# A gated graph network: first block tile by tile, catching up over four blocks, and a new split of low parts in the last layer

## The chip, the cores and the metric

The kernel runs on one core of one Trainium2 chip. The time is the device time of the whole program in microseconds (us); the profile shows one execution of it.

## What is computed

Four layers of a gated graph network on 50,000 nodes with 128 features, and a layer norm over each node's features at the end. With the self loops that the input carries there are 75,000 edges, sorted by destination; 25,000 of the edges are not self loops.

```python
def gru(inp, h):
    i_r, i_z, i_n = split(inp @ w_ih.T + b_ih)
    h_r, h_z, h_n = split(h @ w_hh.T + b_hh)
    r, z = sigmoid(i_r + h_r), sigmoid(i_z + h_z)
    n = tanh(i_n + r * h_n)
    return (1 - z) * n + z * h
h = x
for l in range(4):
    m = h @ weight[l]
    agg = segment_sum(m[src], dst, 50000)
    h = gru(agg, h)
out = layernorm(x + (h + x))
```

## The kernel before

Nodes are taken in 100 blocks of 500 (NB = 100), four to a partition row. A block's state stands transposed, features on partitions and 504 columns (COLS), and each float32 operand of a matmul is split in a high part, rounded on ScalarE (h_hi, g_hi, a_hi), and a low part, the rest, subtracted on VectorE or GpSimd (h_lo, g_lo, a_lo). A product is then three matmuls. weight[l] is folded into w_ih ahead of the loops, so a layer works on the sum of neighbours' states.

A block's other edges lie in three tiles of at most 128 (TILES = 3), one for each third of its rows. GpSimd gathers the sources' rows (gath, L570, three indirect DMAs a block, issued five blocks ahead), and TensorE adds them up by a product with a 0/1 selection (sel) into the PSUM tensor pA (sum_edges, L689: six matmuls of 168 columns). VectorE adds the block's own state (aggT, L1161); in the last layer TensorE does that with two passes through an identity matrix, and aggT does not exist. pA holds one block's sums, so the next sum waits until these are read: for aggT (s_agg), in the last layer for a_lo (s_alo).

Each engine runs an order written out by hand, one step for each block b of each layer, and semaphores tie the engines together. In step b:
- TensorE: r and h_n products on the state of b, r and i_n products on the sums of b, the edge sum of b + 2, the z products of b, the transposes of the new state of b - 1 (L764).
- ScalarE: r gate of b (rg, L892), h_hi and g_hi of b + 3, tanh (L896), a_hi of b + 2, z gate; in the last layer also two halves of the normalised rows of b - 9 (L914), in the others the copy of the rows of b - 2.
- VectorE: narg = h_n times r (L1167), newT of b - 1 (L1193), narg + i_n (L1174), in the last layer the residual sum y_rows of b - 2 (L1202) and its row statistics bn (L1209), in the others aggT of b + 2; then diff = h - n (L1178), g_lo of b + 3 (L1140), in the first three layers the second half of h_lo of b + 3 (L1145), a_lo of b + 2 (L1152), diff times z (L1184). The moments of five blocks are worked out together, once in five steps. In the first layer VectorE also makes the selections (L1129), four blocks ahead.
- GpSimd: h_lo of b + 3 (L550; the first half, in the last layer all 504 columns), the three gathers of b + 5, and in the last layer once in five steps a root for the row norms (L556).
- SP issues loads and stores. Rows go out through a ring of five buffers, o_rows.

A layer's gathers read the rows that the layer before has stored, so its first gather waits for the last store. The steady step has the edge sum two blocks ahead, and a layer begins with none: block 0 is summed alone (L779), the first three steps (RAMP) sum one block ahead, and the third of them sums a second one at its end (L793). The other engines follow with g_hi, g_lo, aggT, a_hi and a_lo in the same places. After the last step the last nine blocks' rows are normalised, the first half of each on ScalarE (L979), the second on VectorE (last_rows, L1317), into o_rows; both wait until the buffer's last store is done.

The branch on flag takes the path described here; general_path is for inputs that don't fit the tables and isn't run.

## Time and profile before

| | |
|---|---|
| median of the three runs | 2383.14 us (lowest 2382.7) |
| the profiled execution's own time | 2381.4 us |
| its span, first to last instruction | 2379.7 us |
| TensorE matmul busy | 2239.1 us (94%) |
| TensorE weight load busy | 1885.0 us (79%) |
| VectorE busy | 2233.1 us (94%) |
| ScalarE busy | 1900.6 us (80%) |
| GpSimd busy | 1724.1 us (72%) |

Matmuls overlap and their ends are modelled, so a TensorE that is busy may still not be at its peak: what it can do is better read from the starts of its instructions. In rows of the time line an instruction's duration holds some 0.09 us after the point at which the next one may start. "issue" is time in which the profile shows nothing that the engine waited for. Names as DVE, ACT, POOL, PE and SP stand for VectorE, ScalarE, GpSimd, TensorE and the SyncE queue.

### The profile page before, as it was taken

Reading aid. Unit: us, or ns where it says so; the run is one execution under the profiler, and the core shown is the slowest. Engines: PE = TensorE matmul, PEld = TensorE weight load, DVE = VectorE, ACT = ScalarE, POOL = GpSimd, SP = SyncE. Lnnn points to the kernel's source line nnn. Section 1 sums busy time; section 2 is a strip of 40 time slices with the busy share of each in tenths; the row PEclk is TensorE's granted clock in tenths of the full one; section 3 lists DMA queues with packets and bytes.
Section 4 is the critical chain, followed back from the end, with each engine's and each line's share of the span. In section 5 each row is a group of like instructions: output and inputs, shape, how many; then the busy total and the mean of one; then the engine's idle time right before and its main releaser. Section 6 shows DMA issues by size and latency. Waiting matters only on the chain.

```text
span 2379.7 us, 49508 instructions
## 1 busy us (share of the span) xinstructions
PE 2239.1 (94%) x11832; PEld 1885.0 (79%) x11832; DVE 2233.1 (94%) x4543; ACT 1900.6 (80%) x3592; POOL 1724.1 (72%) x1645
## 2 busy tenths in 40 slices
PE   2799999999989999999979999999979999999996
PEld 1688888888768888888858888888858888888885
DVE  7799999999879999999969999999969999999998
ACT  1588888888768888888858888888857999999996
POOL 2687777777376777777567777777658888888883
PEclk7899999999989999999989999999989999999998
DMA  2355555555546555555535555555544555555553
GB/s 57 89 158 162 158 161 157 161 157 161 154 115 173 172 172 169 174 172 169 169 112 174 170 173 172 169 172 173 169 124 122 153 151 150 151 151 151 151 152 110
DMA packets 277065, 363.68 MB, mean 153 GB/s; under 512 B 107755, under 2 KB 186587, under 8 KB 276981
## 3 DMA queue, kind: packets, MB, share of 16 engines
q1 hardware_dynamic: 238196, 310.43, 43.7%
q0 software_dynamic: 38784, 52.30, 9.0%
q8 instruction: 32, 0.52, 0.1%
q14 instruction: 53, 0.43, 0.1%
HBM read 209.32 MB, written 179.81 MB: 164 GB/s over the span
## 4 chain that ended last, share of the span: by engine, by line
DVE 48%; issue 29%; PE 10%; ACT 9%; DVEq 2%; DMA 1%; POOL 0%; SPq 0%; ACTq 0%; POOLq 0%
DVE a_lo L1152 9%; DVE narg L1174 8%; DVE diff L1178 5%; DVE h_lo L1145 5%; DVE diff L1184 5%; ACT pA L896 3%; ACT pIN L896 3%; PE pR L717 3%; DVE aggT L1161 3%; DVE sel L1129 3%; PE pA L705 2%; DVE newT L1193 2%; DVE narg L1167 2%; PE pZ L717 2%; DVE bn L1209 2%
## 5 line engine op out<-in xcount | busy, mean ns | idle before, releaser
L570 POOL DMA_INDIRECT gath<-state,idx x900 | 943.6, 1048 | 260.0 <-issue 239.7
L550 POOL TENSOR_TENSOR h_lo<-hT,h_hi 128x252 fp32r<-128x252 f32 (+1 forms) x400 | 351.7, 879 | 247.1 <-ACT h_hi L869 162.6
L570 POOL DMA_INDIRECT gath<-in_x_dram,idx x300 | 345.7, 1152 | 108.6 <-issue 72.1
L892 ACT ACTIVATE rg<-pR,bsum 128x504 f32<-128x504 f32 x400 | 272.5, 681 | 87.3 <-PE pR L717 75.6
L1167 DVE SCALAR_TENSOR_TENSOR narg<-pHN,bhh,rg 128x504 f32<-128x504 f32 x400 | 294.0, 735 | 31.4 <-ACT rg L892 29.6
L705 PE MATMUL pA<-sel,g_hi 128*128 128x168 f32 x1200 | 278.4, 266 | 22.3 <-DVE g_lo L1140 22.3
L705 PE MATMUL pA<-sel,g_lo 128*128 128x168 f32 x1200 | 291.3, 276 | 0.0
L880 ACT CAST sel<-sel 128x504 fp32r (+1 forms) x400 | 246.3, 616 | 34.1 <-DVE flag_i L1136 33.9
L1184 DVE TENSOR_TENSOR diff<-zg,diff 128x504 f32<-128x504 f32 x400 | 270.3, 676 | 0.8 <-DVE diff L1178 0.5
L900 ACT ACTIVATE zg<-pZ,bsum 128x504 f32<-128x504 f32 x400 | 269.9, 675 | 0.0
L1140 DVE TENSOR_TENSOR g_lo<-gath,g_hi 128x384 fp32r<-128x384 f32 x400 | 231.7, 579 | 35.8 <-ACT g_hi L873 35.8
L705 PEld LDWEIGHTS pA<-sel,g_hi 128*128 128x128 f32 x1200 | 231.3, 193 | 41.6 <-issue 25.1
L705 PEld LDWEIGHTS pA<-sel,g_lo 128*128 128x128 f32 x1200 | 231.5, 193 | 16.4
L896 ACT ACTIVATE pA<-narg,bih 128x504 f32<-128x504 f32 x200 | 137.2, 686 | 134.2 <-DVE narg L1174 133.6
L764 PEld LDWEIGHTS pO<-ident,newT 128*125 128x125 f32 x1400 | 197.2, 187 | 56.3 <-DVE newT L1193 30.2
L896 ACT ACTIVATE pIN<-narg,bih 128x504 f32<-128x504 f32 x200 | 137.2, 686 | 127.4 <-DVE narg L1174 126.7
L873 ACT CAST g_hi<-gath 128x384 fp32r<-128x384 f32 x400 | 207.4, 518 | 24.7 <-DMA gath<-state,idx 23.0
L764 PE MATMUL pO<-ident,newT 128*125 128x128 f32 x1400 | 215.3, 276 | 11.0 <-DVE newT L1193 11.0
L1152 DVE TENSOR_TENSOR a_lo<-aggT,a_hi 128x504 fp32r<-128x504 f32 x300 | 203.4, 678 | 2.7 <-ACT a_hi L885 2.7
L1161 DVE TENSOR_TENSOR aggT<-pA,hT 128x504 f32<-128x504 f32 x300 | 200.7, 669 | 5.0 <-PE pA L705 5.0
L885 ACT CAST a_hi<-aggT 128x504 fp32r<-128x504 f32 x300 | 179.4, 598 | 17.2 <-DVE aggT L1161 17.2
L717 PE MATMUL pR<-h_hi,whh_hi 128*128 128x504 f32 x400 | 191.2, 478 | 0.0
(185 smaller groups left out, 6460.7 us busy)
## 6 DMA issues: line engine op xcount, KB each, us to landing
columns<-newT SPq DMA_DIRECT2D x300, 252.0 KB, 2.0
hT<-columns SPq DMA_DIRECT2D x300, 252.0 KB, 2.7
state<-o_rows SPq DMA_DIRECT2D x300, 224.0 KB
x_rows<-in_x_dram SPq DMA_DIRECT2D x200, 224.0 KB
out_dram<-o_rows SPq DMA_DIRECT2D x100, 224.0 KB
gath<-state,idx POOLq DMA_INDIRECT x900
state<-o_rows SPq DMA_DIRECT2D x300, 26.0 KB
idx<-edge_src SPq DMA_DIRECT2D x395, 1.5 KB
```

The costliest lines, as they stand in the source:

```text
L550: nc.gpsimd.tensor_tensor(h_lo[:, u % RING, cols], hT[:, u % RING, cols], h_hi[:, u % RING, cols].bitcast(F32), ALU.subtract).then_inc(s_h ...
L570: pool.indirect_dma_start(out=gath[:, u % RING, j, :], out_offset=None, in_=states[l], in_offset=bass.IndirectOffsetOnAxis(ap=idx[:, u % R ...
L705: last = nc.tensor.matmul(to, rows, cols, start=begins, stop=ends)
L717: last = nc.tensor.matmul(bank, w, xx[:, u % RING, :], start=begins and k == 0, stop=ends and k == len(passes) - 1)
L764: last = nc.tensor.transpose(bank[0:ROWS, k * D:(k + 1) * D], newT[:, u % RING, k * CP:k * CP + ROWS], ident[:, :])
L892: nc.scalar.activation(rg[:, :], pR[:, 0:COLS], ACT.Sigmoid, bias=bsum[:, 0:1]).then_inc(s_r, 1)
L896: nc.scalar.activation(n_bank(u), narg[:, :], ACT.Tanh, bias=bih[:, 2:3]).then_inc(s_n, 1)
L900: nc.scalar.activation(zg[:, :], pZ[:, 0:COLS], ACT.Sigmoid, bias=bsum[:, 1:2]).then_inc(s_z, 1)
L1152: v.tensor_tensor(a_lo[:, u % RING, :], sums_of if summed else aggT[:, :], a_hi[:, u % RING, :].bitcast(F32), ALU.subtract).then_inc(s_alo, 1)
L1161: v.tensor_tensor(aggT[:, :], sums_of, hT[:, u % RING, :], ALU.add).then_inc(s_agg, 1)
L1167: v.scalar_tensor_tensor(narg[:, :], pHN[:, 0:COLS], bhh[:, 2:3], rg[:, :], ALU.add, ALU.mult).then_inc(s_t1, 1)
L1184: v.tensor_tensor(diff[:, :], zg[:, :], diff[:, :], ALU.mult).then_inc(s_e, 1)
```

## The change

**First block, tile by tile.** Each of the three gathers of a layer's block 0 gets its own semaphore. g_hi, g_lo, the two matmuls, aggT, a_hi and a_lo run for each tile (128 gathered columns, 168 block columns) in three PSUM banks (first_sums), by the new functions first_gathered and first_high_part on ScalarE and first_low_gathered, first_aggregate and first_low_part on VectorE, each the old work on a third of the columns.

**Catching up over four blocks.** RAMP is 4. Steps 0 to 2 sum blocks 1 to 3; step 3 sums block 4 between the r and the i_n product and block 5 behind the z products. g_hi, g_lo and a_lo of these blocks, VectorE's part of h_lo and the selections move to match; block 1's g_hi and g_lo, made ahead of step 0 before, are made in it.

**Last layer.** GpSimd makes 378 columns of h_lo (MOST) and VectorE the other 126; the state products and the edge sum wait for both. g_lo of b + 3 stands between the residual sum and the row statistics.

**Ends.** In a layer's last step newT of the block before goes ahead of narg, and h_lo behind the last newT. The last nine blocks are normalised in place, in y_rows, and stored from there: ScalarE takes all columns of the first four of them, and half of the other five; the shift of the earlier group stands ahead of the last moments.

```diff
 HALF = COLS // 2
+MOST = 3 * COLS // 4
...
-RAMP = 3
+RAMP = 4
...
             for k in range(OUTLAG, 0, -1):
-                sp.wait_ge(s_olast, OUTLAG - k + 1)
-                store(l, NB - k, UNROLL - k)
+                if k <= RING:
+                    sp.wait_ge(s_olast, RING - k + 1)
+                store(l, NB - k, UNROLL - k, True)
...
 def split_h(l, b, u, behind=None, whole=False, ready=1):
-    cols = slice(0, COLS if whole or l == L - 1 else HALF)
+    cols = slice(0, COLS if whole else MOST if l == L - 1 else HALF)
...
     if l == L - 1:
         pe.wait_ge(s_hlo, g + 1)
+        pe.wait_ge(s_hlov, g + 1 - PRE)
...
-def products_on_sums(l, b, u, reused):
+def sum_first(l, start):
+    at_least(s_alo if l == L - 1 else s_agg, l * NB, start)
+    if l == L - 1:
+        pe.wait_ge(s_hlo, l * NB + 1)
+        pe.wait_ge(s_hlov, l * NB + 1 - PRE)
+        for j in range(TILES):
+            nc.tensor.matmul(first_sums(j), ident_r[:, :], of_rows(h_hi[:, 0, :], j), start=True, stop=False)
+            nc.tensor.matmul(first_sums(j), ident_r[:, :], of_rows(h_lo[:, 0, :], j), start=False, stop=False)
+    pe.wait_ge(s_sel, l * NB + 1)
+    for j in range(TILES):
+        pe.wait_ge(*of_first(j, s_ghi0, s_ghi, l))
+        nc.tensor.matmul(first_sums(j), g_hi[:, 0, j, :], selection(0, j), start=l < L - 1, stop=False)
+        pe.wait_ge(*of_first(j, s_glo0, s_glo, l))
+        nc.tensor.matmul(first_sums(j), g_lo[:, 0, j, :], selection(0, j), start=False,
...
-            products_on_state(l, b, u, start, l < L - 1 and (l > 0 or exists_before(i, u, PRE)))
+            products_on_state(l, b, u, start, l > 0 or exists_before(i, u, PRE))
             if first:
-                sum_edges(l, 0, 0, start)
+                sum_first(l, start)
                 z_on_state(l, 0, 0, start)
-            products_on_sums(l, b, u, l * NB + b - 1 if l or exists_before(i, u, 2) else None)
-            if exists(i, u, 2):
-                sum_edges(l, *after(i, u, 1 if ramp else 2)[:2], False)
+            r_on_sums(l, b, u)
+            if ramp and u == 3:
+                sum_edges(l, 4, 4, False)
+            n_on_sums(l, b, u, l * NB + b - 1 if l or exists_before(i, u, 2) else None)
+            if ramp and u == 2:
+                sum_edges(l, 3, 3, False)
+            elif not ramp and exists(i, u, 2):
+                sum_edges(l, *after(i, u, 2)[:2], False)
             if first:
                 z_on_sums(l, u)
             else:
                 z_product(l, b, u, start)
+            if ramp and u != 2:
+                nu = 5 if u == 3 else u + 1
+                sum_edges(l, nu, nu, False)
             if not first:
...
+def normalise_in_place(u, shifted, columns):
+    act.wait_ge(s_nmr, shifted)
+    for k in range(columns):
+        row = y_rows[:, u, k * D:(k + 1) * D]
+        last = nc.scalar.activation(row, row, ACT.Identity, bias=nmr[:, u, k:k + 1], scale=rstd[:, u, k:k + 1])
+    last.then_inc(s_o, 1)
 def fast_path():
     for l in range(L):
...
 def low_h(l, b, u):
     dve.wait_ge(s_hhi, l * NB + b + 1)
-    v.tensor_tensor(h_lo[:, u % RING, HALF:COLS], hT[:, u % RING, HALF:COLS],
-                    h_hi[:, u % RING, HALF:COLS].bitcast(F32), ALU.subtract).then_inc(s_hlov, 1)
+    cols = slice(MOST if l == L - 1 else HALF, COLS)
+    v.tensor_tensor(h_lo[:, u % RING, cols], hT[:, u % RING, cols], h_hi[:, u % RING, cols].bitcast(F32),
+                    ALU.subtract).then_inc(s_hlov, 1)
...
             if first:
                 if l == 0:
-                    for j in range(TILES):
-                        select(1, 1, j)
-                low_gathered(l, 0, 0)
-                if l == 0:
-                    for j in range(TILES):
-                        select(2, 2, j)
+                    for c in range(1, RAMP):
+                        for j in range(TILES):
+                            select(c, c, j)
+                first_low_gathered(l, 0)
                 if not final:
-                    aggregate(l, 0, 0, l == 0)
-                low_part(l, 0, 0, final)
-                low_gathered(l, 1, 1)
-                if l == 0:
-                    for j in range(TILES):
-                        select(3, 3, j)
+                    first_aggregate(l, 0, l == 0)
+                first_low_gathered(l, 1)
+                first_low_part(l, 0)
+                if not final:
+                    first_aggregate(l, 1, l == 0)
+                first_low_gathered(l, 2)
+                first_low_part(l, 1)
+                if not final:
+                    first_aggregate(l, 2, l == 0)
+                first_low_part(l, 2)
             added = final and exists_before(i, u, ROWLAG)
             half = half_done(i, u, RING + ROWLAG) if final else None
             shifted = half_done(i, u, OUTLAG) if final else None
+            ramp = isinstance(i, int) and i == 0 and u < RAMP
+            if last:
+                renew(*after(i, u, -1))
             r_times_hn(l, b, u)
+            if ramp and u == 1:
+                low_gathered(l, 2, 2)
             if shifted:
                 shift(*shifted)
-            if not first:
+            if not first and not last:
                 renew(*after(i, u, -1))
             n_argument(l, b, u)
+            if ramp and u == 0:
+                low_gathered(l, 1, 1)
+            if ramp and u == 3:
+                low_gathered(l, 5, 5)
             if added:
                 remainder(*after(i, u, -ROWLAG))
+                if not ramp and exists(i, u, 3):
+                    low_gathered(l, *after(i, u, 3)[:2])
                 row_stats(*after(i, u, -ROWLAG)[:2])
-            ramp = isinstance(i, int) and i == 0 and u < RAMP
             summed = after(i, u, 1 if ramp else 2)[:2] if exists(i, u, 2) else None
+            if ramp and u == 0:
+                difference(l, b, u)
             if not final and summed:
                 aggregate(l, *summed)
             if half:
                 moments(*half, RING * (half[1] + 1))
-            if l == 0 and exists(i, u, 4):
+            if l == 0 and exists(i, u, RAMP) and not ramp:
                 for j in range(TILES):
-                    select(*after(i, u, 4)[:2], j)
-            difference(l, b, u)
+                    select(*after(i, u, RAMP)[:2], j)
+            if not (ramp and u == 0):
+                difference(l, b, u)
             if half:
                 squared_difference(*half)
-            if ramp and u == RAMP - 1:
-                low_gathered(l, RAMP + 1, RAMP + 1)
-            if not ramp and exists(i, u, 3):
+            if not added and not ramp and exists(i, u, 3):
                 low_gathered(l, *after(i, u, 3)[:2])
             coming = on_from(l, i, u, PRE)
-            if coming and coming[0] < L - 1:
+            if coming and not ramp and not last:
                 low_h(*coming[:3])
             if summed:
                 low_part(l, *summed, final)
+            if ramp and u == 3 and not final:
+                aggregate(l, 5, 5)
+            if ramp and u == 2:
+                low_gathered(l, 4, 4)
             product(l, b, u)
+            if coming and ramp:
+                low_h(*coming[:3])
             if half:
                 variance(*half)
-            if ramp and u < RAMP - 1:
-                low_gathered(l, u + 2, u + 2)
-            if ramp and u == RAMP - 1:
-                if not final:
-                    aggregate(l, RAMP + 1, RAMP + 1)
-                low_gathered(l, RAMP + 2, RAMP + 2)
-                low_part(l, RAMP + 1, RAMP + 1, final)
+            if ramp and u == 1:
+                low_gathered(l, 3, 3)
+            if ramp and u == 3:
+                low_part(l, 5, 5, final)
+                low_gathered(l, 6, 6)
+            if l == 0 and ramp:
+                for j in range(TILES):
+                    select(RAMP + u, RAMP + u, j)
             if last:
                 renew(b, u, i)
+                if coming:
+                    low_h(*coming[:3])
         blocks(dve, step)
         if final:
...
                 u = UNROLL - k
                 dve.wait_ge(s_nmr, turn(GROUPS - 1, u) + (1 if k > LATE else 2))
-                dve.wait_ge(s_store[u % RING], 32 * (TURNS * (L - 1) + turn(GROUPS - 1, u)))
                 for c in range(RPP // 2, RPP):
-                    last = v.tensor_scalar(o_rows[:, u % RING, c * D:(c + 1) * D], y_rows[:, u, c * D:(c + 1) * D],
-                                           rstd[:, u, c:c + 1], nmr[:, u, c:c + 1], ALU.mult, ALU.add)
+                    row = y_rows[:, u, c * D:(c + 1) * D]
+                    last = v.tensor_scalar(row, row, rstd[:, u, c:c + 1], nmr[:, u, c:c + 1], ALU.mult, ALU.add)
                 last.then_inc(s_olast, 1)
             ahead = slice(RING, UNROLL - LATE), TURNS - 1
...
             for k in range(LATE, 0, -1):
                 remainder(NB - k, UNROLL - k, GROUPS - 1)
                 row_stats(NB - k, UNROLL - k)
+            shift(*ahead)
             moments(*late, NB)
             squared_difference(*late)
             variance(*late)
-            for k in range(OUTLAG, RING, -1):
-                last_rows(k)
-            shift(*ahead)
             for k in range(RING, LATE, -1):
                 last_rows(k)
             shift(*late)
```

VectorE at the start of the second layer, before: g_lo, aggT and a_lo of block 0, g_lo of block 1, then the steps of blocks 0 and 1.

```order
L1140 TENSOR_TENSOR g_lo<-gath,g_hi 128x384
L1161 TENSOR_TENSOR aggT<-pA,hT 128x504
L1152 TENSOR_TENSOR a_lo<-aggT,a_hi 128x504
L1140 TENSOR_TENSOR g_lo<-gath,g_hi 128x384
L1167 SCALAR_TENSOR_TENSOR narg<-pHN,bhh,rg 128x504
L1174 TENSOR_TENSOR narg<-pIN,narg 128x504
L1161 TENSOR_TENSOR aggT<-pA,hT 128x504
L1178 TENSOR_TENSOR diff<-hT,pIN 128x504
L1145 TENSOR_TENSOR h_lo<-hT,h_hi 128x252
L1152 TENSOR_TENSOR a_lo<-aggT,a_hi 128x504
```

The same place after, from the second tile of block 0 on.

```order
L1271 TENSOR_TENSOR a_lo<-aggT,a_hi 128x4x42
L1264 TENSOR_TENSOR aggT<-pIN,hT 128x4x42
L1271 TENSOR_TENSOR a_lo<-aggT,a_hi 128x4x42
L1278 SCALAR_TENSOR_TENSOR narg<-pHN,bhh,rg 128x504
L1285 TENSOR_TENSOR narg<-pIN,narg 128x504
L1230 TENSOR_TENSOR g_lo<-gath,g_hi 128x384
L1289 TENSOR_TENSOR diff<-hT,pIN 128x504
L1252 TENSOR_TENSOR aggT<-pA,hT 128x504
L1243 TENSOR_TENSOR a_lo<-aggT,a_hi 128x504
L1295 TENSOR_TENSOR diff<-zg,diff 128x504
L1236 TENSOR_TENSOR h_lo<-hT,h_hi 128x252
```

g_lo of block 1 has moved from ahead of the step into it, diff stands ahead of aggT, and h_lo behind the second diff. The next piece is VectorE in a steady step of the last layer, before.

```order
L1193 TENSOR_TENSOR newT<-diff,pIN 128x504
L1174 TENSOR_TENSOR narg<-pA,narg 128x504
L1201 REGISTER_ALU
L1202 SCALAR_TENSOR_TENSOR y_rows<-x_rows,pH 125x512
L1207 REGISTER_ALU
L1209 BN_STATS bn<-y_rows 125x6 x4
L1178 TENSOR_TENSOR diff<-hT,pA 128x504
L1139 REGISTER_ALU
L1140 TENSOR_TENSOR g_lo<-gath,g_hi 128x384
L1152 TENSOR_TENSOR a_lo<-pA,a_hi 128x504
```

And after.

```order
L1304 TENSOR_TENSOR newT<-diff,pIN 128x504
L1285 TENSOR_TENSOR narg<-pA,narg 128x504
L1312 REGISTER_ALU
L1313 SCALAR_TENSOR_TENSOR y_rows<-x_rows,pH 125x512
L1229 REGISTER_ALU
L1230 TENSOR_TENSOR g_lo<-gath,g_hi 128x384
L1318 REGISTER_ALU
L1320 BN_STATS bn<-y_rows 125x6 x4
L1289 TENSOR_TENSOR diff<-hT,pA 128x504
L1236 TENSOR_TENSOR h_lo<-hT,h_hi 128x126
L1243 TENSOR_TENSOR a_lo<-pA,a_hi 128x504
```

g_lo has gone ahead of bn, and 126 columns of h_lo stand where it was. Last, VectorE's end, before.

```order
L1209 BN_STATS bn<-y_rows 125x6 x4
L1214 TENSOR_TENSOR mv<-bn 125x8
L1215 SCALAR_TENSOR_TENSOR mv<-bn 125x8
L1216 TENSOR_TENSOR mv<-bn 125x8
L1220 SCALAR_TENSOR_TENSOR mv<-mv 125x8
L1226 SCALAR_TENSOR_TENSOR veps<-mv 125x8
L1323 TENSOR_SCALAR o_rows<-y_rows,rstd,nmr 125x128 x8
L1232 SCALAR_TENSOR_TENSOR nmr<-mv,rstd 125x12
L1323 TENSOR_SCALAR o_rows<-y_rows,rstd,nmr 125x128 x6
L1232 SCALAR_TENSOR_TENSOR nmr<-mv,rstd 125x8
L1323 TENSOR_SCALAR o_rows<-y_rows,rstd,nmr 125x128 x4
```

And after.

```order
L1320 BN_STATS bn<-y_rows 125x6 x4
L1343 SCALAR_TENSOR_TENSOR nmr<-mv,rstd 125x12
L1325 TENSOR_TENSOR mv<-bn 125x8
L1326 SCALAR_TENSOR_TENSOR mv<-bn 125x8
L1327 TENSOR_TENSOR mv<-bn 125x8
L1331 SCALAR_TENSOR_TENSOR mv<-mv 125x8
L1337 SCALAR_TENSOR_TENSOR veps<-mv 125x8
L1456 TENSOR_SCALAR y_rows<-y_rows,rstd,nmr 125x128 x6
L1343 SCALAR_TENSOR_TENSOR nmr<-mv,rstd 125x8
L1456 TENSOR_SCALAR y_rows<-y_rows,rstd,nmr 125x128 x4
```

The eight pieces for the first four blocks are gone from VectorE, and the first shift (nmr) stands ahead of the last moments.

## Rows read from the trace of the kernel before

**Rows 1.** busy time by stretch: PE, PEld, DVE, ACT, POOL, clock, DMA share, GB/s

```profile
700.00:1100.00 400.00, 400.00 (x2129) 338.48 (x2128) 387.56 (x685) 332.73 (x608) 292.77 (x305) 1.00 0.59 172
1199.00:1216.00 17.00, 8.05 (x23) 5.73 (x23) 2.62 (x5) 4.15 (x8) 10.00 (x10) 0.51 0.23 67
1860.00:2260.00 400.00, 389.90 (x2015) 322.74 (x2015) 389.64 (x888) 362.77 (x740) 346.22 (x283) 1.00 0.55 152
```

**Rows 2.** POOL's waits in the last layer, 1860 to 2260 us: total, times, longest

```profile
POOL gath L570 <- issue: 46.0, 182, 0.3
```

**Rows 3.** groups by line: busy us, mean ns, idle before; last layer, then first

```profile
L1140 DVE TENSOR_TENSOR g_lo<-gath,g_hi 128x384 fp32r<-128x384 f32 x68 | 44.2, 650 | 0.0
...
L550 POOL TENSOR_TENSOR h_lo<-hT,h_hi 128x504 fp32r<-128x504 f32 x67 | 86.2, 1286 | 1.6
...
L550 POOL TENSOR_TENSOR h_lo<-hT,h_hi 128x252 fp32r<-128x252 f32 x62 | 45.7, 737 | 38.8 <-ACT h_hi L859 38.4
```

**Rows 4.** time line, last layer (start, us): VectorE, then GpSimd, then ScalarE

```profile
2002.69 1.06 DVE L1140 TENSOR_TENSOR g_lo<-gath,g_hi 128x384 fp32r<-128x384 f32 x1
...
2006.68 0.67 DVE L1202 SCALAR_TENSOR_TENSOR y_rows<-x_rows,pO 125x512 f32<-125x512 f32 x1
2007.39 0.87 DVE L1209 BATCH_NORM_STATS2 bn<-y_rows 125x6 f32<-125x128 f32 x4
...
2008.76 0.55 DVE L1140 TENSOR_TENSOR g_lo<-gath,g_hi 128x384 fp32r<-128x384 f32 x1
2009.22 0.68 DVE L1152 TENSOR_TENSOR a_lo<-pA,a_hi 128x504 fp32r<-128x504 f32 x1
...
2002.03 1.29 POOL L550 TENSOR_TENSOR h_lo<-hT,h_hi 128x504 fp32r<-128x504 f32 x1
...
2007.27 1.27 POOL L550 TENSOR_TENSOR h_lo<-hT,h_hi 128x504 fp32r<-128x504 f32 x1
...
2003.68 0.67 ACT L892 ACTIVATE rg<-pR,bsum 128x504 f32<-128x504 f32 x1
```

**Rows 5.** time line at the third layer's start: VectorE, GpSimd, ScalarE

```profile
1196.53 0.42 DVE L1145 TENSOR_TENSOR h_lo<-hT,h_hi 128x252 fp32r<-128x252 f32 x1
...
1205.72 0.99 POOL L570 DMA_INDIRECT gath<-state,idx  x1 [0.30 <-issue]
...
1208.23 0.51 ACT L873 CAST g_hi<-gath 128x384 fp32r<-128x384 f32 x1 [7.49 <-DMA gath<-state,idx]
...
1214.99 0.68 ACT L892 ACTIVATE rg<-pR,bsum 128x504 f32<-128x504 f32 x1 [2.09 <-PE pR L717]
```

**Rows 6.** r gates of blocks 0 and 4 by layer; last, a TensorE wait

```profile
77.91 0.68 ACT L892 ACTIVATE rg<-pR,bsum 128x504 f32<-128x504 f32 x1 [0.73 <-PE pR L717]
...
107.01 0.68 ACT L892 ACTIVATE rg<-pR,bsum 128x504 f32<-128x504 f32 x1 [0.45 <-PE pR L717]
...
666.77 0.68 ACT L892 ACTIVATE rg<-pR,bsum 128x504 f32<-128x504 f32 x1 [2.09 <-PE pR L717]
...
692.65 0.68 ACT L892 ACTIVATE rg<-pR,bsum 128x504 f32<-128x504 f32 x1
...
1241.56 0.68 ACT L892 ACTIVATE rg<-pR,bsum 128x504 f32<-128x504 f32 x1 [0.74 <-PE pR L717]
...
1763.56 0.68 ACT L892 ACTIVATE rg<-pR,bsum 128x504 f32<-128x504 f32 x1 [1.41 <-PE pR L717]
...
1790.01 0.68 ACT L892 ACTIVATE rg<-pR,bsum 128x504 f32<-128x504 f32 x1 [0.68 <-PE pR L717]
...
1231.70 0.32 PE L705 MATMUL pA<-sel,g_hi 128*128 128x168 f32 x1 [1.68 <-DVE g_lo L1140]
```

**Rows 7.** time line of the end: ScalarE, then GpSimd

```profile
2358.53 3.95 ACT L914 ACTIVATE o_rows<-y_rows,nmr,rstd 125x128 f32<-125x128 f32 x10
...
2371.29 1.66 ACT L914 ACTIVATE o_rows<-y_rows,nmr,rstd 125x128 f32<-125x128 f32 x4 [0.59 <-DMA out_dram<-o_rows]
...
2365.58 1.67 POOL L556 TENSOR_TENSOR rstd<-veps,mhalf 125x8 f32<-125x8 f32 x1 [1.54 <-DVE veps L1226]
```

121 lines of the change are left out of this document (92 added, 29 removed).

## The prediction

> **What bounds the kernel now.** I read the busy time by stretch first, then each engine's waits, then the time line of a few blocks in each layer. The counts give the length of a block. In the second layer a block has 28 matmuls (18 for the gates, 6 for the edge sums, 4 transposes), and 2129 of them in 400 us make 5.26 us a block [rows 1]. In the last layer a block has 30, and 2015 of them make 5.96 us. There are 100 blocks in each layer, so 0.1 us a block in the last layer is 9 to 10 us of the whole.
>
> In the last layer three engines are near their limit. TensorE's floor is the 5.26 us and two identity passes. The 28 matmuls carry 18 x 504 + 6 x 168 + 4 x 128 columns, so 504 columns take 0.25 us at the full clock, and the floor is at most 5.76. VectorE is busy for 389.6 of 400 us, 5.80 us a block [rows 1]. GpSimd stands between two gathers for 0.30 us each time, and apart from that it waits for nothing: 46.0 us in 182 such pieces, the longest 0.3 us [rows 2]. It works without a break, at 5.96 us a block. Yet no engine waits for GpSimd's results. The tie goes another way: the low part of the gathered rows (g_lo) takes 0.55 us on VectorE in most blocks, but 1.06 us where it starts inside GpSimd's h_lo. In the rows g_lo starts at 2002.69, h_lo runs until 2003.32, and g_lo ends 0.43 us behind it; the next g_lo starts after its h_lo is over and takes 0.55 us [rows 4]. The mean of 650 ns against 550 says that this happens in one block of five [rows 3].
>
> At the start of a layer everything hangs on one chain. Three gathers leave at steps of 1.3 us (0.99 and 0.30), ScalarE waits 7.49 us for the last of them, and the first r gate comes 6.76 us after that (1208.23 to 1214.99) [rows 5]. From there the r gates of blocks 0 to 4 take 29.1, 25.9, 26.6 and 26.4 us in the four layers, where four steady blocks take 21 to 24. One step is long, from block 2 to block 3, where TensorE waits 1.68 us for g_lo of block 4 [rows 6].
>
> **The first block, tile by tile.** Before, 384 gathered columns are split, six matmuls run, and aggT, a_hi and a_lo of 504 columns follow in series. After, only the third tile comes behind the last gather: 128 columns of g_hi and g_lo, two matmuls, 168 columns of aggT, a_hi and a_lo. VectorE's time falls from 0.68 to 0.42 us when columns halve from 504 to 252 [rows 4, 5], so 128 to 168 columns cost about 0.3 us. I take the same on ScalarE. The tail is then five pieces of 0.3 to 0.35 and some 0.65 us of matmuls, since TensorE stands at its lower clock in this stretch (0.51 from 1199 to 1216) [rows 1]. That is 2.4 us behind the last gather. The z product on the state, three matmuls at the lower clock, ends at about the same time, and the r product and gate take 1.8: 4.2 to 4.3 instead of 6.76, 2.5 us less. I take 2.5 for the second and third layer, 2.3 for the first, and 2.0 for the last, which has no aggT to shorten.
>
> **Catching up over four blocks.** The work is the same; the places are new. In the first step g_lo of block 1 is no longer made in the wait before block 0, but behind two narg instructions, so its edge sum starts 2.9 us after the r gate's start (the gate 0.7, three pieces of VectorE at 0.6 to 0.7, and hand-overs). Then come the sum's six matmuls, which I take at 1.3 us at the lower clock and 0.7 at the full, aggT, a_hi, a_lo at 0.7 each and the r product 1.05: 7.4 us. The second step has a gate, g_lo (0.46), newT, narg, aggT, diff and a_lo in series at 0.6 each, with the waits for tanh and a_hi, and the r product: 6.3 us. The third has no g_lo ahead of a_lo: 5.9. The fourth has two edge sums: sum of block 5 waits for g_lo and for aggT of block 4, which are the fourth and fifth piece of VectorE behind the gate, and starts at 3.8; with 0.7 of matmuls, 0.3 for the transposes, 1.4 for the state products and 0.9 for the r product the gate comes after 7.1. The four steps are 26.7 us. In the first layer x is transposed too, 27.2. So the steps give +1.9 (29.1 - 27.2) in the first layer, -0.8 in the second, -0.1 in the third. In the last the fourth step is worse: there the sum of block 5 waits for a_lo of block 4, which stands behind the residual sum, g_lo, four bn and diff; I make it 10.0, and the four steps 28.8 with the identity passes, -2.4. Selections move to the end of a step of VectorE; they fill VectorE's wait for the r gate. SP fetches the indices of blocks 5 and 6 behind the second g_hi, which now comes 1.2 us behind the first r gate; GpSimd has fifteen gathers, 19.5 us, ahead of needing them, so this costs nothing. Starts and steps together: first layer 4.2, second 1.7, third 2.4, last -0.4, **7.9 us**.
>
> **Ends of layers.** In a layer's last step newT of block 98 goes ahead of narg of block 99, into a stretch where VectorE waits for the r gate, and h_lo goes behind newT. The first takes 0.4 us off the chain to the last rows, the second 0.2: 0.6 us, three times, and 0.4 in the last layer: **2.2 us**. Behind h_lo stands only the next layer's first g_lo, which waits for gathers anyway.
>
> **The end of the kernel.** Rows are normalised in place, so no engine waits for a store. ScalarE takes all columns of four blocks: 16 activations at 0.395 (3.95 for 10), from 2358.53 to 2364.9; six for the next three blocks to 2367.3; the last four at 2367.4 behind the root (2365.58 + 1.67) and the shift, to 2369.1. Now its last piece ends at 2372.95 [rows 7]. VectorE keeps ten pieces of eighteen and ends ahead of that. The stores keep their number and behind the last of them nothing changes: **3.8 us**.
>
> **The last layer's steady blocks.** GpSimd's h_lo falls from 504 to 378 columns. It takes 1.286 us for 504 and 0.737 for 252 [rows 3], so 1.01: GpSimd's block falls by 0.27 to 5.69, and it will wait again. VectorE gains a piece of 126 columns: by the slope above 0.29 us long, 0.20 until the next starts. It loses the wait between y_rows and bn: 0.71 us from one to the other now, 0.58 (its 0.67 less the 0.09 by which a_lo overlaps g_lo) if g_lo stands between [rows 4]. Net +0.08. TensorE's new waits for VectorE's quarter (state products and edge sums) cost nothing: the quarter is made a step ahead of the edge sum, in front of an a_lo that this sum waits for anyway. VectorE's floor is 5.80 - 0.10 (no lengthened g_lo) + 0.08 = 5.78, TensorE's 5.76. Now the block is 0.16 above VectorE's busy time; half of that is burst (the moments come once in five blocks and TensorE cannot make up for them), so without any meeting of g_lo and h_lo I get 5.87.
>
> Does it meet? g_lo's new place is right behind y_rows, 3.2 to 3.6 us after the r gate (y_rows starts 3.00 after it, 2006.68 against 2003.68, late by 0.4 in that block). In the same block h_lo starts 3.59 after the gate [rows 4]. With two shorter h_lo ahead of it since the root it will start at about 2.9, and end at 3.9. So g_lo starts inside it and is held up by about 0.6 us, once in five blocks, as now and by as much: 5.96, **0 us**. This rests on 0.3 us of phase.
>
> By the Trainium skill, SBUF — State Buffer, section "SBUF: two separate sides", the port that VectorE and GpSimd share is an exclusive lock: the one that starts first keeps it for its whole instruction and the other fully blocks, and it counts a VectorE instruction with two SBUF inputs. The trace agrees: 0.43 us left of g_lo after h_lo's end. By that rule a g_lo that starts just before h_lo costs VectorE nothing, and one that starts just after pays all of h_lo, 1.0 us: the same meeting is then worth between 0 and 10 to 18 us over the layer.
>
> **Sum.** 7.9 + 2.2 + 3.8 + 0 = 13.9 us off the profiled execution's 2381.4 (span 2379.7), 2367.5. The median of the runs is 2383.1, 1.7 higher. I say **2369**.
>
> **Rivals.**
> - *No meeting in the last layer.* h_lo arrives 0.7 us earlier than I think, or g_lo ahead of it. 5.87 instead of 5.96 in 92 blocks: 8 us more, 2361. For it: the phase is tight. Against: five blocks offer five chances.
> - *GpSimd is the true bound of the last layer.* It is the one engine without a wait [rows 2]. Then relief of 0.27 is passed on until VectorE's floor, 5.78: 17 us more, 2352. Against: nobody waits for it now.
> - *The ramp gives nothing.* The first step's later g_lo, at the lower clock, eats the start in every layer: only ends and tail are left, 6 us, 2377.
> - *Slower in the last layer, and on the whole.* If g_lo meets h_lo in three blocks or more of five, each at 0.6 us, VectorE needs 5.78 + 0.36 = 6.14 with three, 6.26 with four. The layer loses 17 us with three and 28 with four, against 14 gained elsewhere: 2386 and 2397. It decides from 2.5 meetings in five. For it: g_lo's new place is nearer to the gate, where h_lo of an unhurried GpSimd runs (right behind h_hi), the old one stood behind it. Against: after a root h_lo is late in two blocks only.
>
> **Chances.** My forecast 0.40; no meeting 0.22; GpSimd bound 0.10; no gain in the ramp 0.13; slower 0.15. Range 2350 to 2386: from the second rival to three meetings. A measurement tells about 2% (48 us) from no change; none of the cases reaches that on the fast side, and only a meeting in all blocks with a failed ramp on the slow side: faster 0.02, same 0.95, slower 0.03.
>
> **What would show it.** g_lo's mean in the last layer: 650 again if one in five is held up, 550 if none, 900 if three. GpSimd's waits for h_hi, absent now, must appear. The first r gate must come 4.3 us after the third tile's g_hi starts, against 6.76. TensorE's wait of 1.68 must be gone and a longer one for aggT (a_lo in the last layer) stand in the fourth step. ScalarE's last piece ends 6.7 us before the end of the span now; if that distance stays, the tail's gain is whole. I am wrong if block time in layers two and three moves from 5.26, or if the last layer's leaves 5.78 to 6.0.

## The result, and the profile after

The changed kernel took 2389.7 us (median; the kernel before, beside it, 2383.1): a ratio of 1.0029, 95% interval 1.002 to 1.0038. It is 0.3% slower, inside what the forecast called no change, but 20.7 us above the forecast and outside its range. The profile that came with that result was taken at a granted clock of 0.83, so the rows below come from e_changed, the same kernel profiled again at 0.976 beside a kernel before of 2381.2 us (2388.9 us, ratio 1.0032, 1.002 to 1.0045). Its span is 2388.6 us, 8.9 more than the profiled execution of before.

Busy time by stretch, in the order of [rows 1]: PE, PEld, DVE, ACT, POOL, clock, DMA share, GB/s.

```profile
700.00:1100.00 400.00, 400.00 (x2134) 340.73 (x2133) 387.58 (x687) 333.76 (x610) 296.20 (x306) 1.00 0.59 172
1860.00:2260.00 400.00, 381.46 (x1965) 314.08 (x1965) 393.94 (x928) 353.76 (x720) 313.95 (x275) 1.00 0.53 148
```

The second layer is as before. In the last, 1965 matmuls instead of 2015 [rows 1] say that a block got longer. The length of a block is read from r gates; here those of blocks 20 and 90 (start, us, on ScalarE's time line).

```profile
1883.79 0.67 ACT L953 ACTIVATE rg<-pR,bsum 128x504 f32<-128x504 f32 x1
...
2311.88 0.67 ACT L953 ACTIVATE rg<-pR,bsum 128x504 f32<-128x504 f32 x1
```

That is 428.09 us in 70 blocks, 6.116 a block, outside the 5.78 to 6.0 that the forecast allowed; the same two gates of before give 5.965. VectorE's and GpSimd's groups in 1860 to 2260 us (busy us, mean ns | idle before) answer to [rows 3], GpSimd's waits to [rows 2].

```profile
L1230 DVE TENSOR_TENSOR g_lo<-gath,g_hi 128x384 fp32r<-128x384 f32 x65 | 49.4, 761 | 0.0
L1236 DVE TENSOR_TENSOR h_lo<-hT,h_hi 128x126 fp32r<-128x126 f32 x65 | 18.4, 283 | 0.0
L572 POOL TENSOR_TENSOR h_lo<-hT,h_hi 128x378 fp32r<-128x378 f32 x66 | 66.7, 1011 | 35.4 <-ACT h_hi L919 34.8
```

```profile
POOL gath L592 <- issue: 48.9, 183, 0.7
POOL h_lo L572 <- ACT h_hi L919: 34.8, 40, 1.2
```

GpSimd waits again, as forecast, and g_lo's mean has gone up from 650 to 761 ns, between the 650 that the forecast gave for one meeting in five and its 900 for three. The time line of one block (r gate at 2030.82) shows the meeting, beside that of [rows 4].

```profile
2033.55 0.68 DVE L1313 SCALAR_TENSOR_TENSOR y_rows<-x_rows,pO 125x512 f32<-125x512 f32 x1
2034.14 1.60 DVE L1230 TENSOR_TENSOR g_lo<-gath,g_hi 128x384 fp32r<-128x384 f32 x1
2035.67 0.86 DVE L1320 BATCH_NORM_STATS2 bn<-y_rows 125x6 f32<-125x128 f32 x4
...
2034.31 1.01 POOL L572 TENSOR_TENSOR h_lo<-hT,h_hi 128x378 fp32r<-128x378 f32 x1
...
2038.25 0.47 PE L729 MATMUL pA<-h_hi,ident_r 128*128 128x504 f32 x1 [1.14 <-ACT g_hi L924]
```

g_lo starts 3.32 us after the gate and h_lo 3.49. g_lo ends 0.43 us behind h_lo's end, as in [rows 4], but now it waits for the whole of h_lo and not for its last half: 1.60 us against 1.06. In the next step TensorE stands still for 1.14 us ahead of the edge sum (the row names g_hi; this sum's own g_hi was made a step earlier, and a_lo, the last piece that it waits for, ends at 2037.90). The meeting comes once in five blocks: 14 of the 70 between the gates 20 and 90, with a g_lo of 1.62 us on average.

The third layer's start and the end of the kernel, beside [rows 5] and [rows 7]: gathers and gates of ScalarE, then its last pieces and SP's issues.

```profile
1205.51 0.30 ACT L940 CAST g_hi<-gath 128x128 fp32r<-128x128 f32 x1 [0.62 <-DMA gath<-state,idx]
...
1209.64 0.68 ACT L953 ACTIVATE rg<-pR,bsum 128x504 f32<-128x504 f32 x1 [2.15 <-PE pR L741]
```

```profile
2370.24 10.10 ACT L984 ACTIVATE y_rows<-y_rows,nmr,rstd 125x128 f32<-125x128 f32 x26
...
2371.95 11.50 SPq L422 DMA_DIRECT2D out_dram<-y_rows  x18
```

The first r gate comes 4.13 us behind the start of the third tile's g_hi (forecast 4.3; before, 6.76 us behind the one g_hi). ScalarE's last piece ends at 2380.34, 8.3 us ahead of the end and not 6.7: this part's gain is not whole.

### The profile page after: what moved, and what is told of

Read it like the earlier page. It is cut to its first block, busy times and chain, and to the rows that moved or that the text cites. A ratio compares the mean times of both kernels' runs of the same rounds, so it can differ in the third digit from the quotient of the medians.

```text
span 2566.8 us, 49741 instructions
## 1 busy us (share of the span) xinstructions
PE 2433.9 (95%) x11836; PEld 1991.6 (78%) x11836; DVE 2298.5 (90%) x4657; ACT 1910.2 (74%) x3616; POOL 1647.4 (64%) x1645
## 4 chain that ended last, share of the span: by engine, by line
PE 89%; DVE 5%; ACT 2%; issue 2%; DMA 1%; POOL 0%; SPq 0%; ACTq 0%; DVEq 0%; POOLq 0%
PE pR L741 23%; PE pZ L741 22%; PE pA L729 12%; PE pHN L741 11%; PE pO L807 7%; PE pA L741 5%; PE pIN L741 5%; PE pH L693 2%; PE pH L807 1%; DVE narg L1285 1%; ACT rg L953 0%; DVE sel L1179 0%; ACT h_hi L919 0%; DVE narg L1278 0%; DVE a_lo L1243 0%
## 5 line engine op out<-in xcount | busy, mean ns | idle before, releaser
L592 POOL DMA_INDIRECT gath<-state,idx x900 | 926.7, 1030 | 259.0 <-issue 244.6
L572 POOL TENSOR_TENSOR h_lo<-hT,h_hi 128x252 fp32r<-128x252 f32 (+2 forms) x400 | 322.8, 807 | 513.2 <-ACT h_hi L919 327.2
L592 POOL DMA_INDIRECT gath<-in_x_dram,idx x300 | 314.7, 1049 | 108.6 <-issue 71.5
L729 PE MATMUL pA<-sel,g_lo 128*128 128x168 f32 x1188 | 305.2, 285 | 0.0
L729 PE MATMUL pA<-sel,g_hi 128*128 128x168 f32 x1188 | 289.3, 273 | 7.1 <-DVE aggT L1252 4.0
L729 PEld LDWEIGHTS pA<-sel,g_lo 128*128 128x128 f32 x1188 | 245.2, 206 | 21.9
L807 PEld LDWEIGHTS pO<-ident,newT 128*125 128x125 f32 x1400 | 221.9, 195 | 49.7 <-DVE newT L1304 10.7
L807 PE MATMUL pO<-ident,newT 128*125 128x128 f32 x1400 | 236.3, 297 | 8.6 <-DVE newT L1304 8.5
L1230 DVE TENSOR_TENSOR g_lo<-gath,g_hi 128x384 fp32r<-128x384 f32 x396 | 243.7, 615 | 0.4 <-ACT g_hi L924 0.4
L741 PE MATMUL pR<-h_hi,whh_hi 128*128 128x504 f32 x400 | 206.6, 516 | 0.0
```

The costliest lines, as they stand in the source:

```text
L572: nc.gpsimd.tensor_tensor(h_lo[:, u % RING, cols], hT[:, u % RING, cols], h_hi[:, u % RING, cols].bitcast(F32), ALU.subtract).then_inc(s_h ...
L592: pool.indirect_dma_start(out=gath[:, u % RING, j, :], out_offset=None, in_=states[l], in_offset=bass.IndirectOffsetOnAxis(ap=idx[:, u % R ...
L729: last = nc.tensor.matmul(to, rows, cols, start=begins, stop=ends)
L741: last = nc.tensor.matmul(bank, w, xx[:, u % RING, :], start=begins and k == 0, stop=ends and k == len(passes) - 1)
L807: last = nc.tensor.transpose(bank[0:ROWS, k * D:(k + 1) * D], newT[:, u % RING, k * CP:k * CP + ROWS], ident[:, :])
L1230: v.tensor_tensor(g_lo[:, u % 2, :, :], gath[:, u % RING, :, :], g_hi[:, u % 2, :, :].bitcast(F32), ALU.subtract).then_inc(s_glo, 1)
```

## The experiments

The comparisons fell on several chips, of two kinds. On some the kernel before took 2381 to 2383 us, on others 2428 to 2440. I call them the quick and the late chips; what differs on the late ones has a section of its own, below. A ratio is always to the kernel before on the same chip. The block is that of the last layer, from its gates 20 to 90.

| kernel | chip | median, us | ratio (95%) | block |
| --- | --- | --- | --- | --- |
| a_same (changed) | late | 2438.4 | 1.0039 (1.0027-1.0051) | 6.154 |
| a_no_last | late | 2422.5 | 0.9981 (0.9969-0.9992) | 5.960 |
| a_glo_back | late | 2430.0 | 1.0003 (0.9994-1.0013) | 6.062 |
| b_last | late | 2445.2 | 1.0069 (1.0056-1.0082) | 6.134 |
| b_same (before) | late | 2437.9 | 0.9997 (0.9983-1.0011) | 5.965 |
| a_no_split | late | 2454.5 | 1.0054 (1.0039-1.0070) | 6.186 |
| a_no_root | late | 2453.6 | 1.0047 (1.0031-1.0062) | 6.197 |
| c_order | late | 2521.2 | 1.0321 (1.0306-1.0335) | 6.974 |
| a_base (= a_no_last) | quick | 2376.5 | 0.9976 (0.9966-0.9986) | 5.964 |
| c_mid | quick | 2374.9 | 0.9967 (0.9955-0.9979) | 5.951 |
| a_half | quick | 2385.4 | 1.0010 (1.0001-1.0020) | 6.051 |
| b_no_root | quick | 2391.2 | 1.0038 (1.0024-1.0051) | 6.056 |
| d_changed | late | 2452.3 | 1.0052 (1.0034-1.0070) | 6.178 |
| d_split (= a_glo_back) | late | 2445.5 | 1.0020 (1.0005-1.0035) | 6.124 |
| d_place (= a_no_split) | late | 2451.3 | 1.0045 (1.0029-1.0061) | 6.187 |
| e_changed | quick | 2388.9 | 1.0032 (1.0020-1.0045) | 6.116 |
| e_split (= a_glo_back) | quick | 2376.1 | 0.9977 (0.9967-0.9986) | 5.968 |
| e_best | quick | 2372.6 | 0.9966 (0.9952-0.9979) | 5.950 |

### Where the time is: the last layer's two edits

a_no_last undoes both edits of the last layer's steady blocks, a_glo_back only g_lo's new place, and b_last has them alone, on the kernel before.

```diff
# a_no_last
-                cols = slice(0, COLS if whole else MOST if l == L - 1 else HALF)
+                cols = slice(0, COLS if whole or l == L - 1 else HALF)
...
# a_no_last and a_glo_back, in VectorE's step
                             remainder(*after(i, u, -ROWLAG))
-                            if not ramp and exists(i, u, 3):
-                                low_gathered(l, *after(i, u, 3)[:2])
                             row_stats(*after(i, u, -ROWLAG)[:2])
...
-                        if not added and not ramp and exists(i, u, 3):
+                        if not ramp and exists(i, u, 3):
                             low_gathered(l, *after(i, u, 3)[:2])
...
```

In a_no_last VectorE's low_h and TensorE's waits for it are gone from the last layer as well.

> The changed kernel itself, for a profile at an undisturbed clock. It was measured 6 to 7 us slower than before (2389.7 against 2383.1) where 14 us faster was forecast, so 20 us have to be found. Theory L (last layer): the steady blocks of the last layer take 0.2 us more than before, 6.15 to 6.2 instead of 5.96, because g_lo meets h_lo in three or four blocks of five; g_lo's mean there is 850 to 950 ns instead of 650, and GpSimd waits for h_hi. Theory R (ramp): the last layer's block is 5.96 as before, and the r gates of blocks 0 to 4 stand 31 us or more apart in each layer instead of 26 to 29. Either way the last piece of ScalarE ends 6.7 us before the end of the span.

> The changed kernel with both changes of the last layer's steady blocks undone: GpSimd makes all 504 columns of h_lo there and g_lo stands behind diff again. The first block by tiles, the catching up over four blocks, the ends of layers and the end of the kernel stay. Theory L: 14 us less than before, 2369. Theory R: as the changed kernel, 2388 or more.

> The changed kernel with g_lo back behind diff in the last layer; VectorE keeps its quarter of h_lo. It tells which of the two changes of the last layer costs. If it is the new place of g_lo (theory L in its strict form), this one is near the kernel without both, within 4 us, since VectorE's floor is 5.80 - 0.10 + 0.20 = 5.90: 2366 to 2370. If it is the quarter on VectorE, this one is as slow as the changed kernel or slower by the 0.12 us of the wait ahead of bn that comes back, 2389 to 2398.

> The kernel before with the two changes of the last layer alone (378 columns of h_lo on GpSimd, 126 on VectorE, g_lo ahead of bn). Theory L: 20 us slower than before, 2403, with g_lo's mean in the last layer at 850 to 950 ns. Theory R: within 4 us of before, 2380 to 2387, g_lo's mean at 550 to 650.

Without the two edits the changed kernel is faster than before (0.9981), with them slower, and they alone make the kernel before slower (1.0069). So the loss is theirs, and the other edits, taken together, do gain. They gain less than was expected: 5 us and not 14. g_lo's mean in a_same was 757 ns and not 850 to 950, so three or four meetings in five are out too. With g_lo back in its place more than half of the loss is gone, but 7.5 us stay above a_no_last, where 4 were allowed. All this was measured on a late chip; e_changed and e_split repeat it on a quick one.

> The changed kernel once more, since d_changed also ran where the kernel before takes 2440. VectorE's own time was the same there as in a_same (6.01 to 6.02 a block, g_lo of 1.4 to 1.6 us once in five). Theory: where the kernel before takes 2383, idle time falls from 0.14 to 0.16 to about 0.05, because TensorE's increments are on time, and the block is 6.05 to 6.10; ratio to before 1.002 to 1.004. Rival: 6.15 to 6.18 here too, since the idle time comes from the change.

> The changed kernel with g_lo behind the difference, as a_glo_back and d_split (VectorE busy 5.92, block 6.06 and 6.12 there). Theory: VectorE busy 5.90 to 5.92 again; where the kernel before takes 2383 the block is 5.96 to 6.00 and the ratio 0.998 to 1.000, 6 to 9 us less than e_changed, the price of the meeting of g_lo and h_lo. Rival: 6.05 and more, ratio 1.001 or more.

There the split alone costs nothing that shows in the ratio (0.9977 beside a_base's 0.9976 on another quick chip), its block is 5.968 us, and the whole loss of 13 us (1.0032 less 0.9977, where 6 to 9 us were expected) is g_lo's place. VectorE's g_lo in e_split, 1860 to 2260 us:

```profile
L1230 DVE TENSOR_TENSOR g_lo<-gath,g_hi 128x384 fp32r<-128x384 f32 x67 | 36.9, 551 | 0.0
```

No g_lo is held up there. The steps, from one r gate to the next, tell whether the new place costs anything besides the meeting. In this table they are sorted by the block's number modulo five, each a mean of 14 (blocks 20 to 90). The meeting falls into the step of remainder 4, behind its gate, and delays TensorE in the next, of remainder 0.

| us from gate to gate | 0 | 1 | 2 | 3 | 4 |
| --- | --- | --- | --- | --- | --- |
| before | 6.33 | 5.72 | 5.80 | 6.17 | 5.79 |
| e_split | 5.99 | 5.78 | 5.94 | 6.30 | 5.83 |
| e_changed | 6.96 | 5.73 | 5.89 | 6.20 | 5.79 |
| c_mid | 6.27 | 5.72 | 5.80 | 6.16 | 5.80 |

Between e_split and e_changed the one step behind the meeting grows by 0.97 us, and the other four, where g_lo has the same new place and meets nothing, shrink by 0.24 together. So the loss is the meeting and not the place as such. The first two rows show what the split does: it takes 0.34 from the step behind the old meeting and adds 0.37 to the other four. Its piece is not free, it is paid for by the meeting that is gone.

The next table says what VectorE's block is made of: for each piece the time from its start to the next piece's, less the wait between them, as a mean over the blocks 20 to 90.

| us a block | g_lo | h_lo | y_rows | all else | busy | idle | block |
| --- | --- | --- | --- | --- | --- | --- | --- |
| before | 0.573 | 0 | 0.676 | 4.562 | 5.811 | 0.153 | 5.965 |
| e_split | 0.469 | 0.200 | 0.675 | 4.552 | 5.896 | 0.072 | 5.968 |
| e_changed | 0.685 | 0.206 | 0.595 | 4.542 | 6.028 | 0.088 | 6.116 |
| a_half | 0.469 | 0.331 | 0.678 | 4.537 | 6.015 | 0.036 | 6.051 |
| c_mid | 0.469 | 0.066 | 0.677 | 4.563 | 5.775 | 0.176 | 5.951 |

Twice as much of h_lo on VectorE tests whether its time alone decides. g_lo stands behind the difference, as in e_split.

```diff
-MOST = 3 * COLS // 4
+MOST = COLS // 2
...
```

> The changed kernel with g_lo behind the difference, and VectorE making 252 of the 504 columns of h_lo in the last layer instead of 126. With 126 the block was 6.06 with hardly a g_lo held up. Theory (VectorE's busy time plus a fixed 0.14 of idle time sets the block): the piece grows by 0.13 us (0.42 against 0.29), the block to 6.19 and the time by 12 us over the kernel with 126; ratio to before 1.0045 to 1.006. Rival (GpSimd's freedom counts for something): below 1.002.

The piece grew by 0.13 us as expected, the block from 5.968 to 6.051 and not by the whole 0.13: idle time is not fixed at 0.14, it shrinks to 0.04 as VectorE fills up. The theory's 6.19 and its ratio were missed: the 6.06 it set out from belonged to a late chip. The ratio, 1.0010, is the one that the rival gave (below 1.002), but GpSimd's freedom brought no gain either: the block is longer than e_split's. With 6.015 of 6.051 us busy, VectorE bounds a_half. It bounds the others less strictly. From c_mid over before to e_split its busy time rises by 0.12 us (5.775, 5.811, 5.896) and the block by 0.017; the idle time takes up the rest. What sets the block at 5.95 to 5.97 there is not shown.

### What a meeting needs and costs

> The changed kernel with a product in the place of GpSimd's power of -1/2 (so the rows of the last layer are not normalised rightly; nothing else is left out): the 3.6 us piece that makes h_lo late once in five blocks becomes a short one. Theory (one meeting in five blocks, made by the late h_lo): no g_lo of over 1 us is left in the last layer's steady blocks, its mean falls from 744 to 550 ns, and the block from 6.16 to 5.94, 20 us less than the changed kernel; ratio to before about 0.995. Rival (VectorE's extra piece of h_lo, in every block, is the cost): the block falls by less than 0.05 us and the time by less than 5 us. Rival (GpSimd is the bound): same fall as in the first theory, but GpSimd then shows waits in every block; that tells nothing apart, and the length of g_lo does.

> The kernel before with a product in the place of GpSimd's power of -1/2 (the last layer's rows are not normalised rightly; nothing else is left out): GpSimd's block falls by 0.67 us. In the changed kernel the same edit moved h_lo onto the 80-element nmr, which then took 0.86 us instead of 0.18. Theory (VectorE decides, and meetings cost what overlaps): g_lo is 0.55 throughout, 0.10 a block less; h_lo then runs 1.3 to 2.6 us behind the gate, where nmr stands at 1.45, and nmr takes 1.1 us instead of 0.18 once in five blocks, 0.19 a block more: block 6.0 to 6.06, ratio 1.001 to 1.004. Rival (GpSimd bounds the kernel before): with 0.67 us of relief the block falls to TensorE's 5.76 to 5.86, 10 to 19 us less, ratio 0.992 to 0.996.

Both replace one operation, ALU.pow by ALU.mult in GpSimd's root, and so leave out the right scale of the last layer's rows. a_no_root stayed slow and b_no_root got slower, although no g_lo of their steady blocks was held up any more. A row of a_no_root (busy us, mean ns; last layer) and two rows of its time lines show a new meeting:

```profile
L1343 DVE SCALAR_TENSOR_TENSOR nmr<-mv,rstd 125x20 f32<-125x20 f32 x13 | 11.1, 856 | 0.0
```

```profile
2093.18 0.85 DVE L1343 SCALAR_TENSOR_TENSOR nmr<-mv,rstd 125x20 f32<-125x20 f32 x1
...
2093.00 1.00 POOL L572 TENSOR_TENSOR h_lo<-hT,h_hi 128x378 fp32r<-128x378 f32 x1 [0.69 <-issue]
```

nmr has 20 elements in each partition and took 0.18 us elsewhere. h_lo, no longer late behind a root, now runs right behind every r gate, where nmr stands, and nmr waits for its end. In b_no_root, where h_lo takes 1.29, nmr takes 1.14:

```profile
2033.45 1.14 DVE L1232 SCALAR_TENSOR_TENSOR nmr<-mv,rstd 125x20 f32<-125x20 f32 x1
...
2033.27 1.29 POOL L550 TENSOR_TENSOR h_lo<-hT,h_hi 128x504 fp32r<-128x504 f32 x1 [0.95 <-ACT h_hi L869]
```

The block was 6.056 (expected 6.00 to 6.06), with 0.67 us a block of GpSimd's work gone: GpSimd was not the bound of the kernel before. Here the account closes: g_lo gives back 0.10 us a block, nmr takes 0.19 more, and the block grew by 0.09. In a_no_root it does not. g_lo gives back 0.21 and nmr takes 0.14, VectorE is busy for 5.95 us a block, less than in the changed kernel, and its idle time is 0.24, so the block stays at 6.20. The nmr is one part of that; the rest, on a late chip, is open.

The root itself is a GpSimd tensor_tensor with two SBUF inputs, of 20 elements in each partition and 3.58 us. It held up no piece of VectorE that could be seen beside it. In e_changed all 18 full g_lo of the last layer that ran inside a root took 0.54 to 0.56 us, in before 0.55 to 0.56:

```profile
2028.12 0.55 DVE L1230 TENSOR_TENSOR g_lo<-gath,g_hi 128x384 fp32r<-128x384 f32 x1
...
2026.83 3.58 POOL L578 TENSOR_TENSOR rstd<-veps,mhalf 125x20 f32<-125x20 f32 x1
```

A g_lo beside gathers alone was not held up either (0.54 to 0.57 us in before, e_changed and e_split). So it is GpSimd's h_lo that makes a meeting.

a_no_split keeps g_lo's new place and gives GpSimd all 504 columns again.

> The changed kernel with GpSimd making all 504 columns of h_lo in the last layer again; g_lo stays ahead of the row statistics. VectorE's floor falls by 0.2 us a block, GpSimd is back at 5.93 to 5.96 without a wait. Theory (the meeting of g_lo and h_lo sets the cost): the meeting stays, with an h_lo of 1.29 instead of 1.00, VectorE needs 5.58 + 1.2/5 = 5.85 and the layer falls to GpSimd's 5.96 or a little above, 6.0; 15 us less than the changed kernel, ratio to before 0.997 to 0.999. Rival (g_lo ahead of bn delays the TensorE chain by itself, whatever the meeting): 6.10 and above, ratio 1.003 or more.

It was no faster than the changed kernel: 1.0054 here, and beside each other on another late chip 1.0045 (d_place) and 1.0052 (d_changed), where 0.997 to 0.999 was expected. The meetings had moved to the product and to the first of the moments (VectorE, 1900 to 2300 us):

```profile
L1293 DVE TENSOR_TENSOR diff<-zg,diff 128x504 f32<-128x504 f32 x65 | 54.4, 837 | 0.0
...
L1323 DVE TENSOR_TENSOR mv<-bn 125x20 f32<-125x20 f32 x13 | 13.2, 1012 | 0.0
```

Both take two inputs from SBUF, like g_lo, nmr and h_lo; pieces that read PSUM (narg, newT, y_rows, a_lo) kept their mean lengths within 10 ns in all of these kernels. In d_place, the same kernel, the two rows were shorter in the mean (736 and 635 ns) and g_lo's longer (770 ns for 688), VectorE was busy for 5.96 us a block and not 6.11, and the block was the same, 6.187. So VectorE's busy time doesn't explain this kernel's block, and it never ran on a quick chip: what it adds to the case is only where meetings can fall.

### Moving h_lo on GpSimd

```diff
+                        if l == L - 1 and exists(i, u, RING):
+                            ahead = {4: 3, 0: 1}.get(u % RING, 0)
+                        if ahead:
+                            gather(l, b + RING, u, turn(i, u) + 1, True, range(ahead))
...
                             split_h(*coming[:3], l * NB + b if exists_before(i, u, 1) else None)
...
```

> The changed kernel with another order on GpSimd in the last layer, and the same work: in the block behind the one with the root h_lo stands behind all three gathers, and in the block behind that one behind the first gather. Theory: h_lo starts then about 1.5 and 3.8 us after an r gate and no longer at 3.2 to 3.5, beside g_lo; g_lo's mean falls from 744 to about 560 ns, the block from 6.16 to 5.94 to 5.98 and the time by 16 to 20 us against the changed kernel: ratio to before 0.995 to 0.998. Rival (the meeting is made up elsewhere, VectorE's busy time bounds the block): under 5 us. Rival (the h_lo moved meets another VectorE instruction with two SBUF inputs, the product or VectorE's own h_lo): g_lo is short and another row of VectorE gets longer by as much; no gain.

This failed badly, and not by any of the three theories. TensorE's waits, 1860 to 2260 us:

```profile
PE pA L734 <- POOL h_lo L572: 21.3, 7, 3.3
```

The last layer's edge sum of block b+3 takes h_lo of that block through the identity one step after it is split, not three, and I had moved h_lo beyond it. After such waits TensorE also ran at half of its clock: matmuls of 504 columns took 0.62 us instead of 0.39, the mean clock of the run was 0.957. h_lo's lateness has a limit of one step. So this way of moving the meeting out, h_lo behind more gathers, is closed; other orders on GpSimd were not tried.

### A version that beats both

c_mid takes a_base (ramp, hand-overs and tail of the change, no edit in the steady last layer) and lets VectorE make half of h_lo in one block of five, the one in which h_lo is late and met g_lo. e_best does the same but not in the ramp. Its edit against a_base, without VectorE's calls and TensorE's waits for the half:

```diff
+        def shared(l, u, i):
+            return l == L - 1 and u % RING == 2 and not (isinstance(i, int) and i == 0)
...
-                cols = slice(0, COLS if whole or l == L - 1 else HALF)
+                whole = whole or l == L - 1 and not shared(l, u, i)
+                cols = slice(0, COLS if whole else HALF)
...
```

> The changed kernel without both edits of the last layer's steady blocks (GpSimd makes all 504 columns of h_lo, g_lo stands behind the difference as before): ramp, ends of layers and end of kernel alone, the same as a_no_last, run again beside the next three. Every theory: 0.997 to 0.999 of before, block of the last layer 5.96.

> As a_base, but in one block of five, the one behind GpSimd's root, the two engines share h_lo (252 columns each). Theory (a VectorE instruction with two SBUF inputs that overlaps h_lo waits for h_lo's end, and VectorE's time decides): h_lo of that block ends before g_lo starts, the 1.07 us g_lo is gone (0.10 us a block less), VectorE's share costs 0.09 a block; block 5.93 to 5.97, total -3 to +1 us against a_base. GpSimd's cost falls by 0.11 a block. Rival (GpSimd is the true bound in the kernel before): the block falls by 0.1 or more, 9 us. Rival (every piece added to VectorE costs more than its length): block 6.0 or more.

> As c_mid (one block of five shares h_lo between VectorE and GpSimd, g_lo in its old place), but the blocks of the last layer's ramp share nothing, since its fourth step took 11.5 us in c_mid against 9.9 in a_base. Theory: block 5.95 as in c_mid, fourth step 9.9, 1 to 2 us less than c_mid; ratio 0.996 to 0.997 of before. Rival: the fourth step's length has nothing to do with the sharing; ratio as c_mid's 0.9967 or above.

The block of 5.951 is as expected: g_lo gives back 0.104 us, h_lo takes 0.066, the rest of the 0.035 is partly lost to idle time. e_best's fourth step is 9.92 us against 11.52 in c_mid, as expected, its ratio 0.9966 is within the error of c_mid's 0.9967 and of a_base's 0.9976. All three beat the kernel before by 6 to 9 us; which of them is best is not settled, and that e_split is worse is not shown either.

### What the late chips do

> The kernel before, unchanged, as a profile beside the others of this chip. Every theory: a ratio of 1.000 within 0.002. It settles a question of the ramp: the changed kernel showed 13.6 and 9.8 us in its first two steps after a layer's first r gate on another chip than the one of [rows 6]. If those lengths belong to the chip or to the new positions of code, the four steps from rg 0 to rg 4 are here 33 to 38 us too, against 29.1, 25.9, 26.6 and 26.4 in the first trace; if they come with the changed order alone, they stay within 1 us of the first trace.

> The changed kernel as it is, profiled again (the profile of a_same came from a chip on which the kernel before, too, took 2.2% longer, with 0.2 us more in each block of the first layer). Theory: where the kernel before takes 2383, the ramp and the ends gain 6 to 7 us as in a_base and the last layer loses 13: 3 us in its fourth step and 0.10 to 0.11 in each later block, so that the block is 6.07, made of VectorE's 6.01 to 6.03 busy (one g_lo in five at 1.5) and hardly any idle time. Rival: the block is 6.15 as on the other chip, VectorE's idle time stays at 0.14, and the ramp gains more than a_base showed.

> As a_glo_back: the split kept, g_lo behind the difference. With half of h_lo on VectorE (a_half) the block was 6.05 with VectorE busy for 6.015 of it. Theory (VectorE's busy time decides, and its idle time shrinks as it fills up): VectorE busy 5.80 - 0.10 + 0.20 = 5.89 to 5.90, the block 5.97 to 6.02, ratio 0.998 to 1.000. Rival (an added piece costs the same whatever its size, since the extra wait of TensorE is the cost): 6.05 as with the half, ratio 1.001.

> As a_no_split: GpSimd makes all 504 columns, g_lo ahead of the row statistics. Theory: GpSimd has no slack, its late h_lo and root now overlap the product and the first of the moments (0.84 and 1.0 us, as in a_no_split); VectorE's busy time is about 6.1, as there, and the block 6.15 to 6.19; ratio 1.003 to 1.006, more than the changed kernel. Rival (what those long rows showed belonged to the other chip): 5.96 and ratio 0.998.

The kernel before itself needed 36.3, 31.8, 33.3 and 35.3 us for the four ramps on a late chip, and 5.95 us a block in the first layer instead of 5.66. The blocks of its second, third and last layer (5.30, 5.26, 5.965) were the same within 0.04 us. So the long ramps of a_same belong to the chip. ScalarE's waits in the first layer, 116 to 516 us, in b_same and then in the profile of before:

```profile
ACT rg L892 <- PE pR L717: 34.9, 35, 1.4
ACT rg L892 <- issue: 14.9, 31, 0.7
```

```profile
ACT rg L892 <- PE pR L717: 35.1, 70, 0.5
```

A semaphore increment is what tells the next engine that a piece is done. TensorE's increment behind its last r matmul is recorded 0.012 to 0.015 us after the matmul's modelled end in every block of the profiles from quick chips, and so are its other increments. In b_same, first layer, 33 of the 40 that are recorded for the r product came 0.4 to 1.7 us late, and the r gates with them: 38 of 70 start more than 0.25 us behind the product's end, none in before, where it is 0.10 in most. ScalarE's, GpSimd's and nearly all of VectorE's came 0.008 to 0.013 us behind theirs on both. All profiles of late chips showed it and none of a quick one. What causes it is open; as the ends of matmuls are modelled, the profile can't tell a late increment from a matmul that took longer. The last layer of the changed kernel pays for it on such a chip (late increments of the r, n and z products, block 6.154 to 6.178 against 6.116), that of the kernel before does not: there they fall mostly on edge sums and z products, and none on the r product. So a_same overstates the edits, d_changed and d_split missed the blocks expected for a quick chip (6.07 and 5.97 to 6.02), and the split looked as if it cost 0.1 us a block (a_glo_back 6.062, d_split 6.124) where on a quick chip it costs nothing (5.968).

## Why the prediction was wrong, point by point

The account, forecast against e_changed; + is a gain in us.

| part | forecast | measured | from |
| --- | --- | --- | --- |
| start of the first layer | +2.3 | +0.8 | first gate 77.91, 77.1 |
| three hand-overs (starts 7.0, ends 1.8) | +8.8 | +7.9 | last gate to next first: 23.03, 22.52, 22.78; now 19.79, 20.18, 20.48 |
| ramp steps, four layers | -1.4 | -7.3 | 29.1, 25.9, 26.6, 26.4; now 30.5, 26.6, 26.6, 31.5 |
| end of the kernel | +4.2 | +1.9 | last gate to end 25.18; now 23.28 |
| last layer's steady blocks | 0 | -13.2 | gates 4 to 99: 564.5; now 577.7 |
| other steady blocks | 0 | +0.9 | |
| sum | +13.9 | -9.0 | span 2379.7; now 2388.6 |

**What bounds the kernel.** Right: not GpSimd. b_no_root took 0.67 us a block from GpSimd and the kernel got slower. VectorE is right in part: a_half filled it and the block followed, but e_split added 0.085 us of busy time to before and the block grew by 0.003.

**The last layer's steady blocks: the failing step.** "g_lo starts inside it and is held up by about 0.6 us, once in five blocks, as now and by as much: 5.96." Once in five was right. The 0.6 was the mis-sized term: it was 1.08 us, 0.216 a block. In the forecast's own terms 0.6 is 0.12 a block, and 5.87 with it is 5.99 and not 5.96, so 3 of the 13 us were lost in the sum itself.

The phase behind the 0.6 was taken from the wrong block. The forecast worked with the gate at 2003.68 and the second h_lo behind the root, 3.59 us after that gate, and moved it to 2.9. That one came at 2.78 us on average, as forecast, and met nothing, since g_lo came at 4.24 there. The meeting of before is one step earlier, with the first h_lo behind the root: it starts at 2002.03, 4.15 us after its gate, and has no other h_lo between itself and the root.

```profile
1997.88 0.68 ACT L892 ACTIVATE rg<-pR,bsum 128x504 f32<-128x504 f32 x1
...
1994.28 3.57 POOL L556 TENSOR_TENSOR rstd<-veps,mhalf 125x20 f32<-125x20 f32 x1
```

In e_changed this first h_lo starts 3.51 us after its gate and g_lo at 3.32 (means of 14). In before g_lo stood at 4.81, well inside h_lo, and only the rest of h_lo was left; in its new place g_lo stands at h_lo's start, and all of it is left. VectorE's floor without meetings came out at 5.81 (forecast 5.78; the split costs 0.206, y_rows gives back 0.081), its idle time at 0.088 (forecast 0.09). So 5.81 + 0.09 + 0.22 = 6.12. Without this layer's 13.2 us the kernel would have come to some 2376 us, inside the range; a_base, which leaves the two edits out, took 2376.5.

**The rule of the Trainium skill** (SBUF — State Buffer, section "SBUF: two separate sides") says that whichever of the two engines starts first holds the shared port for its whole instruction. The forecast had worked out from it that a g_lo just behind h_lo's start costs 10 to 18 us over the layer and one just ahead of it nothing; 13.2 us were paid, by g_lo that are recorded as starting ahead. The runs agree that VectorE's instructions with two SBUF inputs wait for the end of GpSimd's h_lo, down to a 20-element nmr. They do not bear out, by the recorded starts, that the first to start keeps the port: g_lo began 0.05 to 0.22 us ahead of h_lo in 16 of the 17 meetings behind gate 10 in e_changed, 0.38 in the other, and waited all the same. Nor does all of GpSimd's two-input work block: its root didn't. The forecast had weighed the rule and not let it move the sum.

**Rivals.** "Slower in the last layer" was the true one in sign and size (forecast 2386 with three meetings), by another mechanism: one meeting of the full length. "Three meetings" at 0.6 us had left out the idle time that the block without meetings had; with it they would be 6.23. "No meeting" was refuted by g_lo's mean; "GpSimd is the true bound" by b_no_root; "the ramp gives nothing" was right in size: starts and steps together were forecast at +7.9 and came to -0.4 us (0.8, 7.9 less the 1.8 of the ends, -7.3). The starts were there; longer steps in the first and last layer ate them.

**The first block, tile by tile.** Right: 4.13 us behind the third tile for 4.3, and 3.2, 2.3 and 2.3 us off the three hand-overs (forecast 3.1, 3.1 and 2.6). In the first layer only 0.8 of 2.3 came; why is open.

**Catching up over four blocks.** The steps of the second and third layer were 7.09, 6.30, 5.83 and 7.40 (forecast 7.4, 6.3, 5.9, 7.1), their sums 26.6 for 26.7. In the last layer the fourth step was forecast at 10.0; it was 9.93 in a_base and 9.92 in e_best, but 12.04 in the changed kernel. The same kind of meeting stands in it: VectorE's own 126 columns of h_lo wait for GpSimd's h_lo, narg starts 1.34 us after the gate instead of 0.8, TensorE waits 3.38 us for a_lo (2.84 in a_base), and then its clock falls to 1.2 GHz for 3.4 us (matmuls of 0.62 us), which it didn't in a_base. This part belongs to the split and not to g_lo's place: in e_split the step took 14.04 us, in a_half 13.30. So in the profiled executions the split costs 2 to 4 us in the ramp, although its steady blocks cost nothing.

```profile
1775.44 1.55 DVE L1236 TENSOR_TENSOR h_lo<-hT,h_hi 128x126 fp32r<-128x126 f32 x1
...
1775.82 1.01 POOL L572 TENSOR_TENSOR h_lo<-hT,h_hi 128x378 fp32r<-128x378 f32 x1
...
1782.02 0.70 PE L729 MATMUL pA<-h_hi,ident_r 128*128 128x504 f32 x1 [3.38 <-DVE a_lo L1243]
```

In the first layer the steps were 7.1, 9.1, 5.8 and 8.5, 3.3 us over the forecast of 27.2. The second stands out: ScalarE waits 3.45 us for the r product there. I did not pursue it; the same step took 7.5 to 7.8 in other profiles of quick chips.

**The end of the kernel.** ScalarE ended 3.4 us earlier after the last gate, as forecast (3.8), but "behind the last of them nothing changes" failed: SP issues two stores a block, 0.8 us and more, and the 18 of the last nine blocks took 11.50 us, the longest 1.49 where none had taken over 0.42 before. Its last issue ended 18.1 us after the last gate, before 19.5. ScalarE ends at 2380.34 and SP issues nearly without a break until 2383.45, so SP bounds the new tail, which gave 1.9 us instead of 4.2. Why single issues became longer is open.

## What to carry to other kernels

A VectorE instruction with two SBUF inputs must be priced together with what GpSimd does at that moment: where it overlapped GpSimd's subtraction h_lo, it waited in nearly every case for the rest of it, even a piece of 0.2 us. Read first from a trace which GpSimd work does this: here the 3.58 us root and the gathers did not. Where a forecast hangs on less than a microsecond of phase between two such engines, both ends of that phase belong in the sum, and moving a piece to "a free place" needs a look at every two-input piece near it, since the meeting moves on to the next one. Compare kernels only beside the same chip's own runs of the kernel before, and profile that one too.

## What the hardware showed that I had not expected

- The order of the recorded starts does not decide who waits. A g_lo that starts up to 0.38 us ahead of GpSimd's h_lo waited for it in all of e_changed's steady meetings (g_lo at 2034.14, h_lo at 2034.31), and in d_place four did so that started 0.68 to 0.70 us ahead, longer than the 0.55 us that a free g_lo takes. But in c_mid a g_lo that starts with h_lo was free, and h_lo took 1.13 us instead of 0.73; the same came up once each in eight more of these profiles. What decides is open.

```profile
2325.09 0.55 DVE L1233 TENSOR_TENSOR g_lo<-gath,g_hi 128x384 fp32r<-128x384 f32 x1
...
2325.09 1.13 POOL L573 TENSOR_TENSOR h_lo<-hT,h_hi 128x252 fp32r<-128x252 f32 x1
```

- In e_split a g_lo of the ramp took 2.00 us, with h_lo from 0.58 us behind its start; a gather of GpSimd ended just ahead of that h_lo, and whether it counts is open.

```profile
1774.11 2.00 DVE L1230 TENSOR_TENSOR g_lo<-gath,g_hi 128x384 fp32r<-128x384 f32 x1
...
1774.69 1.00 POOL L572 TENSOR_TENSOR h_lo<-hT,h_hi 128x378 fp32r<-128x378 f32 x1
```

- Two kinds of chip for one program, 2383 and 2428 to 2440 us, that differ in when TensorE's increments arrive and little in the mean granted clock (the kernel before: 0.970 to 0.975 and 0.963 to 0.971).
- Behind TensorE's wait of 3.38 us in e_changed's ramp its clock fell to half for 3.4 us, and behind c_order's waits of about 3 us too: such a stall cost more than its length.
